# Preparing the inputs inside the first attention: one merged stage with loads three slots ahead, and the bf16 remainders subtracted on VectorE

## The chip, the cores and the metric

The kernel runs on one core of a Trainium2 chip. The metric is the device time of one execution in microseconds (us), the median of the runs shown.

## The reference, cut to what matters

`x` and `ctx_2048` are both 64 x 64 x 256 in fp32. Eight residual stages follow one another, an attention and a feed-forward layer four times. The change touches the first attention and what prepares it; the other seven stages stay as they are.

```
x = x + L0_xattn(layernorm(x), ctx_2048, ctx_2048)          # the stage that is changed
# in it: q is split over its 64 rows into 8 heads of 8 rows, likewise k and v
qk = einsum('bdm,bdn->bmn', qh, kh) / sqrt(8)               # 512 heads, 256 x 256 each
ret = einsum('bmn,bcn->bcm', softmax(qk, axis=-1), vh)
x = x + L0_ffn(layernorm(x), ...)                           # then the other stages
...
x = x + L3_xattn(layernorm(x), ctx_2048, decay, ...)        # uses a decayed sum over the 64 rows of ctx
```

So each of the 64 batches has 8 heads whose contraction is only 8 long, and whose scores are 256 by 256. The kernel keeps fp32 accuracy with bf16 matmuls: an fp32 number is written as the sum of three bf16 numbers (a first part, the rounded remainder, and the remainder of that). Nine products of parts, 8 rows each, give a contraction over 72 partitions.

## The kernel before, in words

One core holds all of `x` in SBUF as `X`, 32 tiles of 128 rows (two batches) by 256. Two functions that run one after the other, with a barrier between them, do what the change touches.

`prepare` runs over 8 groups of 4 tiles (512 rows), two groups a loop turn. For a group SyncE loads `X` and the context `C` (L131, L133). VectorE takes mean and variance (L262, L265), GpSimd the root (L192, L193), VectorE normalises into `Z` (L269). ScalarE casts the first bf16 part of `C` and of `Z` (L234, L237). The remainders of `C` are subtracted on GpSimd (L197, L200), those of `Z` on VectorE (L273, L276), and ScalarE casts the second and third parts (L242 to L248). SyncE stores the three parts of both to DRAM scratch, `z_parts` and `context_parts`, 128 KB an issue (L155, L160). TensorE transposes `C` (L214), ScalarE copies it to `CT` (L240), and 16 narrow matmuls a group (L221) build the decayed sums of the last attention.

`row_attention` runs over 64 units of 8 heads; 4 units make a pair of tiles, and 2 units share one load. Its engines go through the same slots, one unit a slot: in slot n TensorE makes the scores of unit n (L502, two matmuls a head, into a ring of three PSUM banks `psS`), and VectorE takes each row's maximum from that bank (L610). GpSimd splits the maxima into three bf16 parts (L461 to L465), TensorE turns them (L512), ScalarE copies them out (L570), and SyncE brings them into rows 72 to 74 of the query tile `Q9` (L376). Three slots later TensorE makes the shifted scores (L524, into two buffers `psT`), ScalarE takes the exponential (L576), and TensorE multiplies by the values (L537); `V9`, copied from `CT` by GpSimd (L451), carries a column of ones for the denominators. Every fourth slot SyncE stores the sums (L384), fetches the denominators (L390), stores their inverses (L394) and brings both back (L400, L402); GpSimd scales and adds to `X` (L470, L473). SyncE also loads the queries of a later group at odd slots (L364, 576 KB) and its keys at even ones (L370, 3 x 192 KB), two slots before their use for the keys. The middle of both functions is a hardware loop.

All semaphore waits are written by hand, and each engine takes its instructions strictly in the order written. All DMAs are issued by SyncE, so a wait in its queue holds back every later transfer.

## Time and profile before

| | |
|---|---|
| median of 3 runs (lowest to highest) | 2002.18 us (1997.76 to 2004.27) |
| the profiled execution | 2001.07 us |
| its span, first to last instruction | 1999.0 us |
| busy: TensorE, VectorE, ScalarE, GpSimd | 68%, 68%, 56%, 25% of the span |
| mean granted TensorE clock | 0.841 of full speed |
| the last instruction of `prepare` is issued at | about 115 us |
| first score matmul of the attention | 134.88 us |

The span is a chain of stages, so the shares of the whole span say little. The stretch from 0 to about 115 us is `prepare`, from there to about 570 us the first attention. A row of the timeline gives the start in us, how long the instructions merged in it took, engine, line, operation, and in brackets how long the engine had stood idle and for whom.

### The profile page before, as it was taken

The page shows a single profiled execution, that of the slowest core. Times are in us where ns is not written, and L with a number is a line of the kernel's source. Part 1 is how long each engine was busy: PE and PEld are TensorE (multiplying, and loading weights), DVE is VectorE, ACT ScalarE, POOL GpSimd, SP SyncE. Part 2 cuts the span into 40 slices and gives each one's busy share as a digit, 9 for nine tenths or more (in the row PEclk, how much of TensorE's full clock was granted, in tenths as well). Part 3 has the DMA queues.
Part 4 walks back from the last instruction along what each step waited for, and adds up shares of the span by engine and source line. Part 5 has one row for each costly group of instructions (what it writes and reads, how often), then busy time and mean ns, then how long its engine had stood idle before and what let it go on. Part 6 is the DMA issues. An engine that isn't in the chain of part 4 may idle for free. (4 is left out here: it accounts for less than half of the span.)

```text
span 1999.0 us, 33980 instructions
## 1 busy us (share of the span) xinstructions
PE 1352.8 (68%) x11677; PEld 867.7 (43%) x11698; DVE 1357.4 (68%) x2850; ACT 1119.1 (56%) x1552; POOL 494.0 (25%) x903
## 2 busy tenths in 40 slices
PE   4338999999929995888705666459999546774111
PEld 4315555555517773455501333336666423442100
DVE  6646888888624443478767999726666477775896
ACT  4515777777712121677635888724444337775554
POOL 4412233333320004111002443100101011112663
PEclk9999999999959997899955666679999877777555
DMA  5652555555430002333210000011111210000111
GB/s 167 206 128 61 122 132 132 129 131 132 98 92 1 0 1 39 62 76 74 44 66 2 0 1 1 0 56 31 38 44 27 87 31 1 1 1 11 43 53 42
DMA packets 96395, 118.12 MB, mean 59 GB/s; under 512 B 29728, under 2 KB 82152, under 8 KB 91660
## 3 DMA queue, kind: packets, MB, share of 16 engines
q1 hardware_dynamic: 96268, 116.46, 23.3%
q8 instruction: 75, 1.23, 0.3%
q14 instruction: 52, 0.43, 0.1%
HBM read 80.07 MB, written 22.88 MB: 52 GB/s over the span
## 5 line engine op out<-in xcount | busy, mean ns | idle before, releaser
L610 DVE TENSOR_REDUCE ratt_nmax<-ratt_psS 128x2 f32<-128x512 f32 x512 | 318.3, 684 | 97.3 <-PE ratt_psS L502 97.0
L576 ACT ACTIVATE ratt_E<-ratt_psT 128x1024 f32<-128x1024 f32 x256 | 255.0, 1023 | 108.3 <-PE ratt_psT L524 108.2
L502 PE MATMUL ratt_psS<-ratt_K,ratt_Q 72*128 72x256 bf16 x1024 | 204.0, 283 | 41.5 <-DMA ratt_K<-context_parts 35.9
L524 PE MATMUL ratt_psT<-ratt_Q,ratt_K 75*128 75x256 bf16 x1024 | 195.7, 274 | 7.2 <-DMA ratt_Q<-ratt_rows 6.9
L502 PEld LDWEIGHTS ratt_psS<-ratt_K,ratt_Q 72*128 72x128 bf16 x1024 | 79.9, 99 | 137.5 <-issue 66.0
L537 PE MATMUL ratt_psO<-ratt_E,ratt_V 128*32 128x256 f32 x2048 | 137.9, 387 | 0.7 <-ACT ratt_E L576 0.7
L524 PEld LDWEIGHTS ratt_psT<-ratt_Q,ratt_K 75*128 75x128 bf16 x1024 | 99.4, 98 | 25.1 <-DMA ratt_Q<-ratt_rows 7.4
L3405 PE MATMUL final_psT<-final_identh,final_Z 128*128 128x128 f16 x64 | 8.2, 309 | 110.6 <-ACT final_Z L3439 110.6
L537 PEld LDWEIGHTS ratt_psO<-ratt_E,ratt_V 128*32 128x32 f32 x2048 | 53.6, 109 | 50.4 <-issue 27.4
L897 ACT COPY sffn_XS<-sffn_psG 128x512 f32<-128x512 f32 x8 | 4.7, 586 | 125.6 <-PE sffn_psG L846 125.6
L2207 PE MATMUL nffn_psH<-nffn_W,nffn_QT 128*128 128x512 bf16 x121 | 53.2, 586 | 30.6 <-ACT nffn_H L2286 20.0
L2761 DVE SCALAR_TENSOR_TENSOR gffn_H<-gffn_psU,gffn_uwu,gffn_S 128x512 f32<-128x512 f32 x64 | 46.0, 745 | 27.9 <-ACT gffn_S L2936 27.1
L2864 PE MATMUL gffn_psG<-gffn_WG,gffn_QT 128*128 128x512 bf16 x120 | 49.2, 495 | 22.7 <-DVE gffn_H L2761 19.2
L461 POOL TENSOR_TENSOR ratt_parts<-ratt_nmax,ratt_zero 128x16 bf16<-128x16 f32 x64 | 17.2, 269 | 178.4 <-DVE ratt_nmax L610 178.4
L863 PE MATMUL sffn_psH<-sffn_XS,sffn_W 128*128 128x256 f32 x256 | 58.6, 388 | 3.8 <-ACT sffn_XS L897 3.8
L2237 PE MATMUL nffn_psO<-nffn_W,nffn_HT 128*128 128x256 bf16 x256 | 46.1, 340 | 21.1 <-DVE all_X L2126 18.1
L872 PE MATMUL sffn_psO<-sffn_W,sffn_H 128*128 128x256 f32 x256 | 57.4, 382 | 4.4 <-ACT sffn_H L907 4.4
L2400 POOL TENSOR_TENSOR all_X<-all_X,satt_bo 128x1024 f32<-128x1024 f32 x8 | 18.9, 2365 | 167.4 <-DVE all_X L2465 167.4
L214 PE MATMUL prep_psC<-all_ident,prep_C 128*128 128x128 f32 x64 | 15.7, 426 | 60.9 <-DMA prep_C<-in_ctx_dram 58.2
L1273 DVE SCALAR_TENSOR_TENSOR gatt_PB<-gatt_psS,gatt_PB 128x512 f32<-128x512 f32 x64 | 41.2, 686 | 22.0 <-PE gatt_psS L1014 21.7
L3405 PEld LDWEIGHTS final_psT<-final_identh,final_Z 128*128 128x128 f16 x64 | 6.2, 140 | 114.2 <-ACT final_Z L3439 83.3
L2578 ACT COPY satt_AT<-satt_psF 128x256 f32<-128x256 f32 x32 | 11.9, 373 | 76.4 <-PE satt_psF L2515 76.4
(472 smaller groups left out, 3739.7 us busy)
## 6 DMA issues: line engine op xcount, KB each, us to landing
ratt_Q<-z_parts SPq DMA_DIRECT2D x32, 576.0 KB
ratt_K<-context_parts SPq DMA_DIRECT2D x96, 192.0 KB
gatt_V<-in_ctx_dram SPq DMA_DIRECT2D x16, 512.0 KB, 6.7
z_parts<-prep_ZS SPq DMA_DIRECT2D x48, 128.0 KB, 2.6
context_parts<-prep_CS SPq DMA_DIRECT2D x48, 128.0 KB, 2.3
head_sums<-ratt_O SPq DMA_DIRECT2D x64, 72.0 KB
all_X<-in_x_dram SPq DMA_DIRECT2D x8, 512.0 KB
prep_C<-in_ctx_dram SPq DMA_DIRECT2D x8, 512.0 KB
```

The lines of the kernel that those rows point to most:

```text
L502: mm = nc.tensor.matmul(psS[:, RING[h], c * D:(c + 1) * D], Q9[0:R, buf, h, k % 2, c * P:(c + 1) * P], K9[0:R, buf, h, k % 2, :], start=Tr ...
L524: mm = nc.tensor.matmul(psT[:, p % 2, e, c, :], K9[0:RM, buf, h, u, c * P:(c + 1) * P], Q9[0:RM, buf, h, u, :], start=True, stop=True)
L537: mm = nc.tensor.matmul(psO[32 * g:32 * g + 32, q, :], V9[:, b, c, q * 4 + g, :], E[:, 2 * b + q, g, c, :], start=(c == 0), stop=(c == KC ...
L576: nc.scalar.activation(E[:, 2 * b + p // 2, 2 * (p % 2):2 * (p % 2) + 2], psT[:, p % 2], ACT.Exp, scale=SCALE).then_inc(exped, 1)
L610: nc.vector.tensor_reduce(nmax[:, k % 2, h, :], psS[:, RING[h]].rearrange("p (c t) -> p c t", c=2), AX.X, ALU.max, negate=True).then_inc(m ...
L863: mm = nc.tensor.matmul(psH[:, f % 2, ff, :], W1[:, k, c * P:(c + 1) * P], XS[:, k, :], start=(k == 0), stop=(k == KC - 1))
L872: mm = nc.tensor.matmul(psO[:, b, :], H[:, c, b * P:(b + 1) * P], W2[:, c, :], start=(c == 0), stop=(c == FC - 1))
L1273: v.scalar_tensor_tensor(half, heads.psS[:, r].rearrange("p (h t) -> p h t", t=L), float(DH) ** -0.5, half, ALU.mult, ALU.mult).then_inc(h ...
L2207: nc.tensor.matmul(psH[:, j % 2, cols], QT[:, g % 2, k, j * P:(j + 1) * P], W1[:, k, cols], start=(k == 0), stop=False)
L2237: mm = nc.tensor.matmul(psO[:, j % 2, 0:D], HT[:, j % 2, n, :], W2[:, n, :], start=(n == 0), stop=(n == FF // P - 1))
L2761: v.scalar_tensor_tensor(H[:, g % 2, j, h * HALF:(h + 1) * HALF], psU[:, h, :], uwu[:, g % 2, j:j + 1], S[:, h, :], ALU.mult, ALU.mult).th ...
L2864: nc.tensor.matmul(psG[:, h, :], QT[:, g % 2, k * G + j, :], WG[:, k, cols], start=(k == 0), stop=(k == KC - 1))
```

## The change

`prepare` and `row_attention` become one function, `first_attention`, with one set of slots, written out without hardware loops. It begins 12 slots (`LEAD`) before the first unit. A pair of tiles (256 rows) takes the place of the group of four, and the preparation of pair a is spread over the slots that `at(n, r)` names: step r of pair a stands in slot 4a - 12 + r. Its loads stand at r = -3, three slots before its first step. The steps: 1 turn the context on TensorE and copy it (into `psT`, the ring of the shifted scores) and take statistics; 2 aggregate, first part of C, its remainder; 3 root, second part of C; 4 normalise, third part of C, weigh; 5 first part of Z, sums; 6 remainder of Z, second part of Z; 7 third part of Z. The stores follow one slot behind each part (3 to 5 for C, 6 to 8 for Z).

Other work moves between engines: all remainders are subtracted on VectorE, the second parts are cast by GpSimd, the third part is written directly by the subtraction, the normalisation moves to ScalarE, and the decayed sums go from TensorE to GpSimd (a product) and VectorE (a sum). `CS`, `ZS` and `Z` have one buffer each where `prepare` had two of the parts; `C` keeps two. Lines below are those of the kernel before where they begin with a minus.

```
-def prepare(nc, io, X, CT, ident, zq, ck, ST, wsum):
...
-def row_attention(nc, io, X, CT, ident, identb, zq, ck, o_dram, r_dram):
+def first_attention(nc, io, X, CT, ident, identb, zq, ck, o_dram, r_dram, ST, wsum):
...
+    LEAD = 12
...
+        C = s.sb("C", [P, 2, 2, D])
+        Z = s.sb("Z", [P, 2, D])
+        CS = s.sb("CS", [P, 3, 2, D], BF16)
+        ZS = s.sb("ZS", [P, 3, 2, D], BF16)
...
+        def at(n, r):
+            a, left = divmod(n + LEAD - r, 4)
+            return a if left == 0 and is_pair(a) else None
...
+                def load_c(a):
+                    if a > 1:
+                        sp.wait_ge(c_third, a - 1)
...
+                def load_q(g):
+                    pair, b = g // 2, g % 2
+                    sp.wait_ge(z_out, pair * 48 + 48)
...
+                for n in range(-LEAD - 3, UNITS + 11):
+                    if at(n, -3) is not None:
+                        load_x(at(n, -3))
+                        load_c(at(n, -3))
                     if is_unit(n - 1):
+                        bring_row(n - 1)
+                    if n % 2 and is_unit(n + 3):
+                        load_q((n + 3) // 2)
+                    if n % 2 == 0 and is_unit(n + 2):
+                        load_k((n + 2) // 2)
...
+                    for part in range(3):
+                        if at(n, 3 + part) is not None:
+                            store_c(at(n, 3 + part), part)
+                        if at(n, 6 + part) is not None:
+                            store_z(at(n, 6 + part), part)
...
+                def second_of_z(a):
+                    pool.wait_ge(z_rest, a + 1)
+                    gp.tensor_copy(ZS[:, 1], Z[:]).then_inc(z_second, 1)
...
+                def turn_context(a):
+                    j = job["turn", a]
+                    pe.wait_ge(c_in[a % 2], a // 2 * 16 + 16)
+                    if j > 1:
+                        pe.wait_ge(exped, j - 1)
+                    for k in range(KC):
+                        for t in range(2):
+                            mm = nc.tensor.transpose(psT[:, j % 2, 0, k, t * P:(t + 1) * P],
+                                                     C[:, a % 2, t, k * P:(k + 1) * P], ident[:])
...
+                def first_of_z(a):
+                    act.wait_ge(z_done, a * 2 + 2)
+                    if a > 0:
+                        act.wait_ge(z_out, a * 48)
+                    sc.copy(ZS[:, 0], Z[:]).then_inc(z_first, 1)
+                def first_of_c(a):
+                    act.wait_ge(c_in[a % 2], a // 2 * 16 + 16)
+                    if a > 0:
+                        act.wait_ge(c_out, a * 48)
+                    sc.copy(CS[:, 0], C[:, a % 2]).then_inc(c_first, 1)
...
+                def rest_of_c(a):
+                    dve.wait_ge(c_first, a + 1)
+                    dve.wait_ge(written, job["turn", a] + 1)
+                    v.tensor_tensor(C[:, a % 2], C[:, a % 2], CS[:, 0], ALU.subtract).then_inc(c_rest, 1)
```

VectorE's order in the attention, before: eight maxima a unit, and every fourth unit a reciprocal, nothing else.

```order
L610 TENSOR_REDUCE ratt_nmax<-ratt_psS 128x2 x96
L619 RECIPROCAL ratt_inv<-ratt_inv 128x64
L610 TENSOR_REDUCE ratt_nmax<-ratt_psS 128x2 x32
L619 RECIPROCAL ratt_inv<-ratt_inv 128x64
```

The same engine after, over one pair of tiles in the middle of the attention (L574 are the maxima, L581 the reciprocal).

```order
L574 TENSOR_REDUCE ratt_nmax<-ratt_psS 128x2 x8
L566 TENSOR_TENSOR ratt_CS<-ratt_C,ratt_CS 128x512
L574 TENSOR_REDUCE ratt_nmax<-ratt_psS 128x2 x8
L542 BN_STATS ratt_stats<-all_X 128x6 x2
L570 TENSOR_REDUCE all_ST<-ratt_product 128x2x4
L574 TENSOR_REDUCE ratt_nmax<-ratt_psS 128x2 x8
L549 BN_AGGR ratt_mv<-ratt_stats 128x2 x2
L562 TENSOR_TENSOR ratt_C<-ratt_C,ratt_CS 128x512
L553 TENSOR_TENSOR ratt_Z<-ratt_Z,ratt_ZS 128x512
L574 TENSOR_REDUCE ratt_nmax<-ratt_psS 128x2 x8
L581 RECIPROCAL ratt_inv<-ratt_inv 128x64
L557 TENSOR_TENSOR ratt_ZS<-ratt_Z,ratt_ZS 128x512
```

Between each unit's eight maxima and the next unit's now stand one to four instructions of the preparation; the two subtractions L562 and L553 stand behind one another in the third of the four slots.

SyncE's order before, around the slot that stores the sums (L384).

```order
L376 DMA ratt_Q<-ratt_rows 3x8x128 x2
L370 DMA ratt_K<-context_parts 24x4096 x3
L384 DMA head_sums<-ratt_O 9x4x512 x4
L376 DMA ratt_Q<-ratt_rows 3x8x128 x2
L364 DMA ratt_Q<-z_parts 72x1x4096
L390 DMA ratt_inv<-head_sums 128x1x64
L376 DMA ratt_Q<-ratt_rows 3x8x128 x2
```

The same place after (L214 are the rows, L207 the keys, L221 the sums, L199 the queries, L226 the denominators).

```order
L214 DMA ratt_Q<-ratt_rows 3x8x128 x2
L207 DMA ratt_K<-context_parts 24x4096 x3
L231 DMA inverse_sums<-ratt_inv 128x64
L221 DMA head_sums<-ratt_O 9x4x512 x4
L185 DMA context_parts<-ratt_CS 16x8x512
L190 DMA z_parts<-ratt_ZS 16x8x512
L174 DMA all_X<-in_x_dram 128x2x256
L180 DMA ratt_C<-in_ctx_dram 128x2x256
L214 DMA ratt_Q<-ratt_rows 3x8x128 x2
L199 DMA ratt_Q<-z_parts 72x1x4096
L226 DMA ratt_inv<-head_sums 128x1x64
L185 DMA context_parts<-ratt_CS 16x8x512
```

Behind the sums' stores now stand a pair's second store of C and last store of Z, then the loads of a later pair, and only then the next unit's rows; the last store of C stands behind the query load and the denominators.

ScalarE's order after, over the same four slots from the one with the normalisation (L477 exponential, L491 and L470 the copies of values and rows).

```order
L498 ACTIVATE ratt_Z<-all_X,ratt_shift,ratt_rstd 128x256 x2
L477 ACTIVATE ratt_E<-ratt_psT 128x1024 x2
L491 COPY ratt_O<-ratt_psO 128x2x256
L483 COPY all_CT<-ratt_psT 128x2x256
L477 ACTIVATE ratt_E<-ratt_psT 128x1024
L470 COPY ratt_rows<-ratt_psS 48x128
L477 ACTIVATE ratt_E<-ratt_psT 128x1024
L505 CAST ratt_ZS<-ratt_Z 128x512
L477 ACTIVATE ratt_E<-ratt_psT 128x1024 x2
```

A cast that waits for the stores of the pair before (L505, and one slot later L511 for C) now stands between one unit's last exponential and the next unit's first.

## Rows read from the trace of the kernel before

**Rows 1.** Stages by windows: us, busy PE, PEld, DVE, ACT, POOL, PEclk, DMA, GB/s.

```profile
0.00:60.00 60.00, 22.22 (x104) 21.95 (x105) 37.43 (x73) 30.31 (x35) 23.39 (x30) 1.00 0.58 175
300.00:400.00 100.00, 98.04 (x1043) 59.33 (x1040) 81.11 (x133) 74.83 (x97) 34.19 (x104) 1.00 0.55 131
```

**Rows 2.** Timeline, from the end of the preparation to the first shifted scores.

```profile
111.44 3.85 SPq L160 DMA_DIRECT2D context_parts<-prep_CS  x6
...
123.69 1.50 SPq L370 DMA_DIRECT2D ratt_K<-context_parts  x3
...
134.88 3.17 PE L502 MATMUL ratt_psS<-ratt_K,ratt_Q 72*128 72x256 bf16 x12 [32.67 <-DMA ratt_K<-context_parts]
...
157.13 0.61 PE L524 MATMUL ratt_psT<-ratt_Q,ratt_K 75*128 75x256 bf16 x2 [6.90 <-DMA ratt_Q<-ratt_rows]
```

**Rows 3.** Timeline of ScalarE, VectorE and TensorE over two slots of the attention.

```profile
327.40 1.02 ACT L576 ACTIVATE ratt_E<-ratt_psT 128x1024 f32<-128x1024 f32 x1 [0.17 <-PE ratt_psT L524]
...
329.38 1.94 ACT L576 ACTIVATE ratt_E<-ratt_psT 128x1024 f32<-128x1024 f32 x2 [0.96 <-PE ratt_psT L524]
...
331.39 0.38 PE L524 MATMUL ratt_psT<-ratt_Q,ratt_K 75*128 75x256 bf16 x2
...
333.58 1.02 ACT L576 ACTIVATE ratt_E<-ratt_psT 128x1024 f32<-128x1024 f32 x1 [0.17 <-PE ratt_psT L524]
...
334.91 2.48 DVE L610 TENSOR_REDUCE ratt_nmax<-ratt_psS 128x2 f32<-128x512 f32 x4 [0.84 <-PE ratt_psS L502]
...
335.81 0.38 PE L502 MATMUL ratt_psS<-ratt_K,ratt_Q 72*128 72x256 bf16 x2
```

**Rows 4.** Timeline: the first context has landed.

```profile
7.16 1.05 ACT L234 CAST prep_CS<-prep_C 128x1024 bf16<-128x1024 f32 x1 [2.95 <-DMA prep_C<-in_ctx_dram]
```

**Rows 5.** Lines before 640 us, the prices: busy us, mean ns, idle before.

```profile
L200 POOL TENSOR_TENSOR prep_CR<-prep_CR,prep_CS 128x1024 f32<-128x1024 f32 x8 | 17.0, 2121 | 34.5 <-ACT prep_CS L242 34.5
...
L214 PE MATMUL prep_psC<-all_ident,prep_C 128*128 128x128 f32 x64 | 15.7, 426 | 60.9 <-DMA prep_C<-in_ctx_dram 58.2 <-ACT all_CT L240 2.7
...
L273 DVE TENSOR_TENSOR prep_ZR<-prep_Z,prep_ZS 128x1024 f32<-128x1024 f32 x8 | 9.8, 1226 | 8.9 <-ACT prep_ZS L237 8.9
...
L262 DVE BATCH_NORM_STATS2 prep_stats<-all_X 128x6 f32 x24 | 8.4, 407 | 0.0
L237 ACT CAST prep_ZS<-prep_Z 128x1024 bf16<-128x1024 f32 x8 | 8.4, 1044 | 35.5 <-DVE prep_Z L269 35.5
...
L193 POOL TENSOR_TENSOR prep_rstd<-prep_veps,prep_mhalf 128x4 f32<-128x4 f32 x8 | 8.1, 1012 | 0.6
```

**Rows 6.** Page: DMA issues, KB each, median us to landing.

```profile
z_parts<-prep_ZS SPq DMA_DIRECT2D x48, 128.0 KB, 2.6
context_parts<-prep_CS SPq DMA_DIRECT2D x48, 128.0 KB, 2.3
```

**Rows 7.** Timeline of SyncE over the same two slots.

```profile
324.93 2.73 SPq L384 DMA_DIRECT2D head_sums<-ratt_O  x4
327.76 1.51 SPq L376 DMA_DIRECT2D ratt_Q<-ratt_rows  x2
329.57 0.90 SPq L364 DMA_DIRECT2D ratt_Q<-z_parts  x1
330.86 0.61 SPq L390 DMA_DIRECT2D ratt_inv<-head_sums  x1
```

**Rows 8.** Two single lines: L390's time to landing, and L269's durations (min/median/max).

```profile
DMA to landing us min/median/max: 2.0/4.8/5.4
...
L269 DVE TENSOR_SCALAR prep_Z<-all_X,prep_mv,prep_rstd x32: 399/402/2206, 9.7 to 102.3; 128x256 f32 x24, 128x256 f32<-128x256 f32 x8
```

**Rows 9.** Windows of 1 us around the query load of Rows 7.

```profile
330.00:331.00 1.00, 1.00 (x19) 0.42 (x16) 1.00 (x3) 1.00 (x2) 0.00 (x0) 1.00 0.09 21
...
334.00:335.00 1.00, 1.00 (x17) 0.54 (x10) 0.16 (x2) 0.61 (x1) 0.69 (x3) 1.00 0.38 87
335.00:336.00 1.00, 1.00 (x11) 0.88 (x10) 1.00 (x2) 0.43 (x1) 0.57 (x3) 1.00 0.03 7
```

**Rows 10.** Timeline: a GpSimd and a VectorE subtraction side by side in the preparation.

```profile
93.14 2.12 POOL L200 TENSOR_TENSOR prep_CR<-prep_CR,prep_CS 128x1024 f32<-128x1024 f32 x1 [4.34 <-ACT prep_CS L242]
94.00 2.34 DVE L276 TENSOR_TENSOR prep_ZR<-prep_ZR,prep_ZS 128x1024 f32<-128x1024 f32 x1 [1.74 <-ACT prep_ZS L244]
```

More of the change, by code:

```diff
@@ L427, in _ @@
[L427 to L434 removed]
+                        to = o_dram.rearrange("a (w g) c m -> a g c w m", g=4)[a, g]
@@ new lines, in _ @@
+                gp.memset(flip[:], 0.0).then_inc(ready, 1)
+                gp.memset(ones[:], 1.0).then_inc(ones_set, 1)
+                pool.wait_ge(ready, 7)
+                for n in range(2):
+                    gp.affine_select(out=flip[:], in_=flip[:], compare_op=ALU.not_equal, fill=1.0,
+                                     base=1 - L - n * L, pattern=[[1, L]], channel_multiplier=1).then_inc(ready, 1)
+                    pool.wait_ge(ready, 8 + n)
+                gp.memset(zero[:], 0.0).then_inc(v_set, 1)
@@ L485, in _ @@
-                slots(pool, slot, UNITS + 14)
+                        split_max(n - 1)
+                    if n % 4 == 1 and is_pair(n // 4 - 4):
+                        scale_and_add(n // 4 - 4)
+                    if at(n, 3) is not None:
+                        root(at(n, 3))
+                        second_of_c(at(n, 3))
+                    if at(n, 4) is not None:
+                        weigh(at(n, 4))
+                    if at(n, 6) is not None:
+                        second_of_z(at(n, 6))
@@ L562, in _ @@
-                slots(pe, slot, UNITS + LAG + 1)
+                            turn_max(n - 1)
             @block.scalar
             def _(act):
-                def row(u, b, half):
-                    act.wait_ge(turned, u + 1)
-                    if past(u, 2):
-                        act.wait_ge(row_in[b], half * 32)
-                    nc.scalar.copy(rows[:, b, :], psM[0:6 * NH0]).then_inc(row_out, 1)
-                def exp(m, b, p):
-                    act.wait_ge(shifted, m * 4 + (p + 1))
-                    if p == 0 and past(m, 2):
-                        act.wait_ge(pv, m - 1)
-                    nc.scalar.activation(E[:, 2 * b + p // 2, 2 * (p % 2):2 * (p % 2) + 2], psT[:, p % 2], ACT.Exp,
-                                         scale=SCALE).then_inc(exped, 1)
@@ L579, in leave, with row @@
[L579 to L588 removed]
+                sc = nc.scalar
+                def row(n):
+                    act.wait_ge(turned, n + 1)
+                    if n > 1:
+                        act.wait_ge(row_in[n % 2], n // 2 * 32)
+                    sc.copy(rows[:, n % 2, :], psM[0:6 * NH0]).then_inc(row_out, 1)
@@ L589, in slot @@
+                sc.activation(keep[:, 0:1], decay[:], ACT.Exp, scale=-1.0).then_inc(expd, 1)
+                for n in range(-LEAD, UNITS + LAG + 1):
                     m = n - LAG
```

672 lines of the change are left out of this document (306 added, 366 removed).

## The prediction

> **What bounds the kernel now.** I read the windows by stage first, then the timeline across the border between the two functions, then one period of four slots engine by engine. In the preparation no engine is near full: VectorE is busiest with 37.43 of 60 us, TensorE has 22.22 [rows 1]. In the attention TensorE is busy 98.04 of 100 us, VectorE 81.11, ScalarE 74.83, GpSimd 34.19, the DMA engines 0.55 [rows 1]. So the attention is bound by TensorE, and the preparation by its chain of small steps. Between them lies a border: the last store is issued by 115.3 us, the first keys are issued by 125.19, the first score runs at 134.88, and the first shifted score at 157.13 after waiting 6.90 us for its rows [rows 2]. A slot takes 333.58 - 327.40 = 6.18 us from one unit's last exponential to the next one's [rows 3], four of them 24.7.
>
> **What the change removes.** The first score no longer waits for all 16 pairs, only for pair 0 and for what is queued ahead of it. Its chain: context and statistics wait for the load and the weights, done by 7.2 us [rows 4]. Then transposes 1.0, a copy and the first part of C 0.52 each (half of L237's 1044 ns), remainder 0.62 (half of L273), second part on GpSimd 1.1 (half of L200, the nearest row; no row shows such a cast), third part 0.62 [rows 5], two loads and the store 1.5, landing 2.3 [rows 6]: 15.4 us. CS has one buffer, so C's first part of pair 1 waits for that landing; and since VectorE takes C of pair 1 ahead of Z of pair 0, Z of pair 0 waits too: 0.52 + 0.62 + 0.62, GpSimd's Z part 1.1, root 1.8 (1012 ns and three small ones), C part 1.1, third part 0.6: 21.8. Store, loads and landing of Z 4, query and key issue 2.4, landing near 4: 32 us. Bounds: 26, if the root (1.8) is done while others wait and the Z store and the keys land 2.0 sooner each, and 46, if the first keys take the 9.7 us that they took from the end of their issue (125.19) to the first score [rows 2]. Saved: 134.9 - 32 = 103 us (89 to 109). Of the 6.90 us for the first rows I take 4 as gone (0 to 6.9): behind the first loads now stand fewer transfers. Together 107.
>
> **What it adds to a period.** Pairs 3 to 15 prepare beside running units: 13 periods. I call the four slots A (the sums are stored), B, C and D; B is the one whose last exponential starts at 327.40 [rows 3].
>
> *Transposes (B).* 64 took 15.7 us [rows 5], so four take 1.0 on the engine that bounds. 0.5 if half falls into its own waits, 1.5 if the extra job in the ring of two psT buffers holds the next one up. I take 1.0. The 128 narrow matmuls for the sums leave TensorE, but from a stage where it had time: nothing.
>
> *First part of Z (end of B).* ScalarE now waits there until all Z stores of the pair before have landed, with every later exponential behind it. SyncE issues the last of these behind the sums' stores, which end at 324.93 + 2.73 = 327.66 [rows 7]; two stores of 0.64 each (six took 3.85) [rows 2], and 2.6 to land [rows 6]: 331.5. ScalarE's slot B ends at 327.40 + 1.02 = 328.4, with the transposes 329.4. It waits, casts 0.52, and starts slot C's exponentials at 332.0 in place of 329.38 + 1.0. That is 1.6 late; the shifted score that needs the first of them stood at 331.39, 1.0 after that one's end (half of the 1.94) [rows 3]. TensorE loses 0.6. It is 0 if the store lands a microsecond sooner, and about 3 if it lands as L390's load does, at 4.8 (median) to 5.4 us [rows 8].
>
> *Remainder of C (end of C).* SyncE in slot B: the stores end at 328.9, two loads 0.9, rows 1.5, then the query load waits for the same landing, 331.5; query 0.9, denominators 0.6 [rows 7], last store of C 0.64: 333.6. Its data stand behind the 576 KB of the query, which before was issued by 330.5 and kept the DMA engines busy until about 334.5 [rows 7, 9]: landing near 336.9. ScalarE's slot C ends at 333.58 + 1.02 + 1.6 = 336.2; it waits 0.7, casts 0.52: 337.4. VectorE waits for that cast, then subtracts twice, 2 x 0.62, and only then takes slot D's first maximum, at 338.7 in place of 334.91 + 1.6 = 336.5. The score that needs that bank free starts at 335.81, 0.28 after the first maximum's end (0.62 long, a quarter of 2.48) [rows 3]; so 2.2 - 0.3 = 1.9 lost. Bounds 0.5 (the landing is early; the cast and two subtractions remain) and 4.4 (it comes 2.5 later).
>
> *The rest of VectorE.* B gains two statistics and a sum, 0.7 + 0.6; A and D a subtraction of 0.62 each [rows 5]. VectorE has 0.84 idle in a slot ahead of a first maximum [rows 3], which hides A and D; B overruns by a few tenths. I take 0.5 (0 to 2.3). ScalarE's copy and normalisation and GpSimd's casts fall into idle time: nothing, if GpSimd's split of the maxima is not late; what it costs otherwise is in the bounds of VectorE.
>
> Sum: 1.0 + 0.6 + 1.9 + 0.5 = 4.0 a period, 13 x 4.0 = 52 us. The keys are not late next: SyncE is done with B by 333.6, before slot C's rows are ready, so C's keys are issued no later than now. The loop's end had held SyncE and TensorE up by tenths only; written out, I count it as nothing.
>
> The profiled execution took 2001.1: 2001.1 - 107 + 52 = 1946. It lies 1.1 under the median of 2002.2, so 1947 is the forecast, 2.7% faster. Its own range, from the bounds that are near: 1932 to 1962.
>
> **A page against the rows.** L276, which starts at 94.00 beside L200 on GpSimd (93.14 to 95.26), took 2.34 us where the same subtraction in L273 took 1226 ns; a normalisation L269 took up to 2206 ns against a median of 402 [rows 5, 8, 10]. "SBUF — State Buffer" of the Trainium skill (section "SBUF: two separate sides") says that VectorE with two SBUF inputs and GpSimd share a port pair which the first to start holds for its whole instruction. By that rule the trace agrees, and moving subtractions to VectorE makes them a party to it. It becomes the second rival below.
>
> **Rivals.**
>
> 1. *The covers hold: only the transposes and half a microsecond remain.* For it: the DMA engines are down to 0.09 when the sums have been stored [rows 9], so the stores may land early enough. Against: the two subtractions behind a fresh cast stand in the order whatever the landing. 13 x 1.5 = 20: 2001.1 - 107 + 20 = 1914, with the median 1915.
> 2. *VectorE is held by GpSimd.* A subtraction that meets a GpSimd instruction waits for most of it, as L276 did by 1.1 us [rows 5, 10]. Two such a period, beyond the cover, make 2.3: 13 x 2.3 = 30, so 1977. For it: GpSimd gains two casts and a product a pair. Against: in the order GpSimd waits for the subtraction itself in slot C, and so is idle beside it.
> 3. *Slower: the single buffers make each landing a stall.* ZS and CS cannot be written before three stores have landed, and ScalarE stands in front of all exponentials while it waits. The loss passes the 107 saved at 107 / 13 = 8.2 us a period, 4.2 more than I count. Both landings add in full once ScalarE is waiting, so it decides from 2.1 us more each, that is 4.7 for Z. For it: L390's load takes 4.8 in this very stretch [rows 8], and the first rows waited 6.90 behind loads [rows 2]. Against: these stores took 2.6 beside a DMA share of 0.58, higher than the attention's 0.55 [rows 1, 6]. With 2.5 more each it is 9.0 a period: 2001.1 - 107 + 117 = 2011, median 2012.
> 4. *The early start doesn't come.* The three leading pairs wait for one another's landings, and the first score comes at 46 or later, and the rows wait as before: 18 of the saving lost, 1965. For it: all in one SyncE queue. Against: the units run once pair 0 is there. It is mostly inside my range.
>
> **How the numbers follow.** Forecast 0.52 (1947), rival 1 0.15 (1915), rival 2 0.12 (1977), rival 3 0.11 (2012), rival 4 0.10 (1965). A change of under 0.3%, 6 us, can't be told from none here. From rivals 2 and 3 I leave some chance near the old time: same 0.03, slower 0.10, faster 0.87. The range of 8 in 10 is 1914 to 1988: it leaves out rival 3 and a tail of rival 1.
>
> **What would show it.** The first score near 32 us (26 to 46); a period of four units at 24.7 + 4.0 = 28.7 us while pairs are prepared and 24.7 in the last ones; four transposes in B; ScalarE waiting for `z_parts` at the end of B by about 2 us and for `context_parts` at the end of C by under 1; VectorE's gap before D's first maximum; the first attention ending some 55 us earlier; every later stage as long as now. Wrong it is if the first score comes after 46, if a period is under 26 or over 32 us, or if the stalls stand on GpSimd or on the keys.

## The result, and the profile after

Over 20 runs of each on one chip the changed kernel took 2006.15 us (median; 1993.16 to 2014.65) and the kernel before 1998.76 (1994.68 to 2005.13). The ratio is 1.0031, with a 95% interval of 1.002 to 1.0042: slower by 0.3%, where 2.7% faster was forecast. The profiled execution took 2004.2 us (span 2002.5) against 2001.07 (span 1999.0).

| | before | forecast | changed kernel |
|---|---|---|---|
| first score, us | 134.88 | 32 (26 to 46) | 33.79 |
| first shifted score, us | 157.13 | 50 (157.13 - 107) | 51.08 |
| mean period of four units while pairs are prepared, us | 25.1 | 28.7 | 34.2 |
| ScalarE's last copy of the first attention, us | 556.85 | some 55 earlier | 559.84 |
| granted TensorE clock, 300 to 400 us | 1.00 | (not treated) | 0.85 |

The mean period is the distance between SyncE's loads of the numerators (`ratt_num`), one a pair, over ten pairs: (490.20 - 148.08) / 10 after, (488.03 - 236.72) / 10 before. All that follows the first attention takes as long as it did: its end moved by 3.0 us and the whole by 3.1.

The two scores in the changed kernel's timeline answer to [rows 2]. The start came 106 us earlier, as forecast (107):

```profile
33.79 3.18 PE L387 MATMUL ratt_psS<-ratt_K,ratt_Q 72*128 72x256 bf16 x12 [17.01 <-DMA ratt_K<-context_parts]
...
51.08 0.64 PE L405 MATMUL ratt_psT<-ratt_Q,ratt_K 75*128 75x256 bf16 x2
```

The window of the changed kernel that answers to [rows 1] (columns as there). TensorE is busy 84.98 us of 100 in place of 98.04, at a granted clock of 0.85 in place of 1.00; VectorE and ScalarE, which were given the added work, are busy less than before too. Something holds everything up:

```profile
300.00:400.00 100.00, 84.98 (x769) 48.41 (x771) 70.93 (x124) 61.45 (x86) 37.96 (x98) 0.85 0.55 134
```

Where TensorE loses its time is told by the sums of its own waits between 100 and 420 us (engine, what it does, what it waits for, us, times, longest). The kernel before hardly waits for the maxima (first line); the changed kernel waits 3.8 us a time for them, and 1.2 for the exponentials:

```profile
PE ratt_psS L502 <- DVE ratt_nmax L610: 1.1, 3, 0.6
...
PE ratt_psS L387 <- DVE ratt_nmax L574: 34.1, 9, 5.1
...
PE ratt_psT L405 <- ACT ratt_E L477: 10.5, 9, 1.7
```

What holds it up stands in the timeline of the two slots that answer to [rows 3] and [rows 7]: the end of slot B (312), of slot C (319) and the start of slot D. Columns: start, us, engine, line, operation, and in brackets the idle time ahead of it and what ended it.

```profile
301.26 0.68 DVE L566 TENSOR_TENSOR ratt_CS<-ratt_C,ratt_CS 128x512 bf16<-128x512 f32 x1
...
308.11 1.47 SPq L190 DMA_DIRECT2D z_parts<-ratt_ZS  x1
...
312.27 0.62 ACT L505 CAST ratt_ZS<-ratt_Z 128x512 bf16<-128x512 f32 x1 [3.45 <-DMA z_parts<-ratt_ZS]
...
313.87 0.39 PE L405 MATMUL ratt_psT<-ratt_Q,ratt_K 75*128 75x256 bf16 x2 [1.74 <-ACT ratt_E L477]
...
314.24 0.60 SPq L185 DMA_DIRECT2D context_parts<-ratt_CS  x1
316.28 1.55 SPq L214 DMA_DIRECT2D ratt_Q<-ratt_rows  x2
...
319.24 0.62 ACT L511 CAST ratt_CS<-ratt_C 128x512 bf16<-128x512 f32 x1 [2.07 <-DMA context_parts<-ratt_CS]
319.89 0.69 DVE L562 TENSOR_TENSOR ratt_C<-ratt_C,ratt_CS 128x512 f32<-128x512 f32 x1 [3.33 <-ACT ratt_CS L511]
320.50 0.68 DVE L553 TENSOR_TENSOR ratt_Z<-ratt_Z,ratt_ZS 128x512 f32<-128x512 f32 x1
321.10 2.48 DVE L574 TENSOR_REDUCE ratt_nmax<-ratt_psS 128x2 f32<-128x512 f32 x4
321.25 0.61 POOL L312 CAST ratt_ZS<-ratt_Z 128x512 bf16<-128x512 f32 x1 [11.32 <-DVE ratt_Z L553]
321.85 0.60 PE L387 MATMUL ratt_psS<-ratt_K,ratt_Q 72*128 72x256 bf16 x2 [1.79 <-DVE ratt_nmax L574]
...
327.79 1.57 SPq L214 DMA_DIRECT2D ratt_Q<-ratt_rows  x2
```

Read it from the last store of C at 314.24. It lands at 319.2; ScalarE has waited 2.07 us for it and casts; VectorE has waited 3.33 us for the cast, subtracts twice and only then, at 321.10, comes to slot D's first maximum; TensorE has waited 1.79 us for that maximum, less than in any other period (3.1 to 5.1 us in the ten others between 100 and 460 us). GpSimd stands behind VectorE's second subtraction as well, 11.32 us, with a copy of values and a split of maxima queued behind; the list of waits has none of TensorE for the rows that this split leads to. And the data of that store were ready at 301.94 already, when VectorE had written the third part (L566). From one unit's rows to the next (L214) it takes 11.51 us here, 316.28 to 327.79, where one slot took 6.18 before. Five of the 9.1 us that the period grew are in this one slot.

These stores land later than those of [rows 6] (the page's issues: KB each, median us to landing):

```profile
context_parts<-ratt_CS SPq DMA_DIRECT2D x48, 128.0 KB, 4.9
z_parts<-ratt_ZS SPq DMA_DIRECT2D x48, 128.0 KB, 4.9
```

And TensorE's granted clock, the column ahead of the DMA share in windows of 1 us, falls in this period at 316, behind TensorE's idle time at the end of slot B, and comes back in slot D:

```profile
313.00:314.00 1.00, 0.13 (x2) 0.12 (x3) 0.00 (x0) 1.00 (x2) 0.00 (x0) 1.00 0.14 38
...
316.00:317.00 1.00, 1.00 (x16) 0.35 (x8) 0.56 (x3) 1.00 (x3) 0.00 (x0) 0.63 0.94 236
317.00:318.00 1.00, 1.00 (x8) 0.51 (x5) 0.00 (x0) 0.18 (x1) 0.00 (x0) 0.50 0.56 145
...
325.00:326.00 1.00, 1.00 (x7) 0.69 (x6) 0.68 (x1) 0.40 (x1) 0.85 (x3) 0.50 0.04 12
...
327.00:328.00 1.00, 1.00 (x17) 0.59 (x20) 1.00 (x2) 1.00 (x3) 0.00 (x0) 1.00 0.00 0
```

In between, TensorE works at 1.2 GHz in place of 2.4: a pair of score matmuls takes 0.60 us in place of 0.38, and the line "TensorE is busy" hides it.

This period is the exception. The clock falls eleven times between 100 and 460 us, and the ten other times it falls while TensorE waits at the end of slot C, as in the period around 386:

```profile
386.00:387.00 1.00, 0.00 (x0) 0.00 (x0) 0.00 (x0) 0.10 (x1) 0.00 (x0) 1.00 0.48 111
387.00:388.00 1.00, 0.00 (x0) 0.00 (x0) 0.45 (x1) 1.00 (x2) 0.00 (x0) 0.97 0.89 270
388.00:389.00 1.00, 0.00 (x0) 0.00 (x0) 1.00 (x3) 0.45 (x1) 0.08 (x1) 0.50 0.95 219
```

### The profile page after: what moved, and what is told of

It reads as the page before. It is cut to its first block and busy times, and to the rows that moved or that the text cites. A ratio compares the mean times of both kernels' runs of the same rounds, so it can differ in the third digit from the quotient of the medians.

```text
span 2002.5 us, 32075 instructions
## 1 busy us (share of the span) xinstructions
PE 1372.6 (69%) x11551; PEld 856.8 (43%) x11572; DVE 1356.8 (68%) x2881; ACT 1104.0 (55%) x1568; POOL 516.8 (26%) x983
## 5 line engine op out<-in xcount | busy, mean ns | idle before, releaser
L574 DVE TENSOR_REDUCE ratt_nmax<-ratt_psS 128x2 f32<-128x512 f32 x512 | 322.6, 685 | 89.4 <-PE ratt_psS L387 84.4
L477 ACT ACTIVATE ratt_E<-ratt_psT 128x1024 f32<-128x1024 f32 x256 | 256.7, 1024 | 106.0 <-PE ratt_psT L405 105.8
L387 PE MATMUL ratt_psS<-ratt_K,ratt_Q 72*128 72x256 bf16 x1024 | 220.0, 302 | 70.1 <-DVE ratt_nmax L574 46.4
L405 PE MATMUL ratt_psT<-ratt_Q,ratt_K 75*128 75x256 bf16 x1024 | 211.7, 293 | 13.9 <-ACT ratt_E L477 13.9
L387 PEld LDWEIGHTS ratt_psS<-ratt_K,ratt_Q 72*128 72x128 bf16 x1024 | 85.7, 104 | 172.2 <-DVE ratt_nmax L574 100.3
L429 PE MATMUL ratt_psO<-ratt_E,ratt_V 128*32 128x256 f32 x2048 | 157.5, 431 | 0.7 <-ACT ratt_E L477 0.7
L405 PEld LDWEIGHTS ratt_psT<-ratt_Q,ratt_K 75*128 75x128 bf16 x1024 | 105.5, 105 | 41.3 <-ACT ratt_E L477 18.2
L864 PEld LDWEIGHTS sffn_psH<-sffn_XS,sffn_W 128*128 128x128 f32 x256 | 49.2, 195 | 12.5 <-issue 3.0
L344 POOL TENSOR_TENSOR ratt_parts<-ratt_nmax,ratt_zero 128x16 bf16<-128x16 f32 x64 | 23.1, 360 | 122.1 <-DVE ratt_nmax L574 122.1
```

The lines of the kernel that those rows point to most:

```text
L387: mm = nc.tensor.matmul(psS[:, RING[h], c * D:(c + 1) * D], Q9[0:R, buf, h, n % 2, c * P:(c + 1) * P], K9[0:R, buf, h, n % 2, :], start=Tr ...
L405: mm = nc.tensor.matmul(psT[:, j % 2, e, c, :], K9[0:RM, buf, h, u, c * P:(c + 1) * P], Q9[0:RM, buf, h, u, :], start=True, stop=True)
L429: mm = nc.tensor.matmul(psO[32 * g:32 * g + 32, q, :], V9[:, m % 2, c, q * 4 + g, :], E[:, m % 2 * 2 + q, g, c, :], start=(c == 0), stop=( ...
L477: sc.activation(E[:, m % 2 * 2 + p // 2, 2 * (p % 2):2 * (p % 2) + 2], psT[:, j % 2], ACT.Exp, scale=SCALE).then_inc(exped, 1)
L574: v.tensor_reduce(nmax[:, n % 2, h, :], psS[:, RING[h]].rearrange("p (c t) -> p c t", c=2), AX.X, ALU.max, negate=True).then_inc(maxed, 1)
L864: mm = nc.tensor.matmul(psH[:, f % 2, ff, :], W1[:, k, c * P:(c + 1) * P], XS[:, k, :], start=(k == 0), stop=(k == KC - 1))
```

## The experiments

Twelve kernels, run beside the kernel before. Periods are mean periods as above, over the first ten pairs whose loads are seen. The runs were on three occasions, on which the kernel before took 2002.2 to 2002.8 (1998.76 in the result above), so kernels of different occasions are best compared by their ratios. Period and clock are those of the one profiled execution, which lies up to 12 us off the kernel's median (e8): spread over 13 periods that is 0.9 us, so a difference of under 1 us between two periods can be chance.

| run | edit | time, us | ratio to before (95%) | period, us | clock 300:400 |
|---|---|---|---|---|---|
| (changed kernel) | | 2006.15 | 1.0031 (1.002 to 1.0042) | 34.2 | 0.85 |
| e1_parts | a semaphore for each store of ZS and CS | 1938.96 | 0.9696 (0.968 to 0.9713) | 28.4 | 0.98 |
| e2_parts_z | the same for ZS alone | 2011.41 | 1.0054 (1.0032 to 1.0075) | 34.1 | 0.89 |
| e3_parts_c | the same for CS alone | 1945.94 | 0.972 (0.9704 to 0.9736) | 29.4 | 0.98 |
| e4_fill | matmuls without use where TensorE idles | 1993.72 | 0.9953 (0.9935 to 0.9972) | 33.2 | 0.90 |
| e5_order_c | C's last store one slot earlier | 1945.94 | 0.9723 (0.9697 to 0.9749) | 28.9 | 1.00 |
| e6_later | e1, and C's remainder a slot later | 1925.62 | 0.9615 (0.9581 to 0.9648) | 27.5 | 0.97 |
| e7_pool | the subtractions on GpSimd | 1947.64 | 0.9735 (0.9708 to 0.9763) | 28.4 | 0.98 |
| e8_loads0 | loads at the pair's own slot | 1988.83 | 0.9931 (0.9907 to 0.9955) | 31.9 | 0.88 |
| e9_rest_later | C's remainder a slot later, alone | 1944.93 | 0.9719 (0.9687 to 0.975) | 28.8 | 0.97 |
| e10_best | e6, and the sums' stores a slot earlier | 1915.54 | 0.9567 (0.9544 to 0.9591) | 27.1 | 0.98 |
| e11_best2 | e10, and the loads one slot ahead | 1919.3 | 0.9587 (0.9558 to 0.9617) | 26.9 | 1.00 |
| e12_act_queue | C's last store from ScalarE's queue | 1963.33 | 0.981 (0.9786 to 0.9834) | 30.3 | 0.95 |

### Take the landing waits away: e1, e2, e3

The waits can go without another buffer: a first cast needs only the first store's place to be free, and that store was issued two slots before the third.

```diff
-                        act.wait_ge(c_out, a * 48)
+                        act.wait_ge(c_out[0], a * 16)
+                        act.wait_ge(c_rest, a)
```

GpSimd's and VectorE's writes wait for the second and third store likewise, and SyncE's loads for all three.

> The changed kernel with one edit: each of the three stores of ZS and of CS gets its own semaphore, so the first cast of a pair waits only for the first store of the pair before (issued two slots earlier), not for all three. Theory A (ScalarE stands before its casts until the last store has landed, 35.0 us in 12 waits for z_parts and 29.0 in 13 for context_parts, and TensorE's idle behind it lets the granted clock fall): both waits go to under 0.3 us a period, the granted clock is 1.00 from 120 to 560 us as in the kernel before, the period of four units falls from 33.0 to 27 to 28 us (24.7 + 1.0 of transposes + about 2 of subtractions behind a fresh cast), 13 periods x 5 to 6 = 65 to 78 us: 2006 becomes 1928 to 1945. Theory B (the added work on VectorE and TensorE fills the slots, the landings only show where the time would be lost anyway): period 31 to 33, time 1985 to 2006. Theory C (the wait moves to the query loads, which need all three stores): ScalarE's waits go, TensorE waits for ratt_Q by as much, time 1985 or more.

Measured: 1938.96, inside theory A's 1928 to 1945; both waits are gone from the list. The period of 28.4 and the clock of 0.98 just miss what it said. B and C fall. The window (columns as above):

```profile
300.00:400.00 100.00, 90.72 (x937) 53.81 (x938) 85.34 (x151) 75.50 (x102) 45.16 (x118) 0.98 0.68 162
```

> The same edit for ZS alone, so that the wait for context_parts at the end of slot C stays. Theory A with stalls that each carry their own fall of the clock: the period falls by about half of what both edits give, to 30 us, time 1965 to 1972. If one stall is enough to hold the clock down for half of the period: only the 2.2 us of the wait itself go, period 31, time 1975 to 1982, and both edits together give more than the sum of the two alone. Theory B: 1995 to 2006.

> The same edit for CS alone, so that the wait for z_parts at the end of slot B stays. Theory A with stalls that each carry their own fall of the clock: period 30 us, time 1965 to 1972. If the Z stall alone takes the clock down (it falls at 316, four microseconds behind TensorE's idle at 312 to 314, and before the C stall begins): the clock stays under 0.9 in this kernel, period 30.5 to 31, time 1975 to 1982, while the edit for ZS alone gives more. Theory B: 1995 to 2006.

Measured: 2011.41 for ZS alone, 1945.94 for CS alone. Neither form of theory A had this: the two stalls are not halves. Without the Z wait ScalarE is at C's cast earlier, and the store that it waits for lands no earlier, so that wait takes the time. The sums of the waits between 100 and 420 us (columns as above), first of the changed kernel:

```profile
ACT ratt_CS L511 <- DMA context_parts<-ratt_CS: 22.8, 9, 3.7
```

then of e2_parts_z:

```profile
ACT ratt_CS L517 <- DMA context_parts<-ratt_CS: 39.3, 9, 6.2
```

That is 2.5 us a time before the edit and 4.4 after; TensorE's wait for the maxima grows with it, from 34.1 us in 9 to 50.5 in 9. Without the C wait (e3), the Z wait stays, 31.1 us in 11, and costs 29.4 - 28.4 = 1.0 us a period against e1 in the profiled executions; the medians differ by 7 us, which makes 0.5. The clock of e3 is 0.98, so the Z stall alone doesn't hold it down. So the fault is at the end of slot C.

### What the clock costs: e4

```diff
+    FILL = (14, 14)
...
+                            if (n % 4, p, e) == (3, 1, 1) and is_unit(n) and is_unit(m):
+                                fill(psO[:, 1, :], n, FILL[1])
                             if is_unit(n):
                                 score(n, 2 * p + e)
+                            if (n % 4, p, e) == (2, 2, 0) and is_unit(n) and is_unit(m):
+                                pe.wait_ge(maxed, n * NH0 + 3)
+                                fill(psS[:, 2, 0:D], n, FILL[0])
```

> The changed kernel with both waits left in, and 14 matmuls of 256 columns without use (into banks that are free at the time) in TensorE's queue at each of its two idle places of a period: 14 x 0.11 = 1.5 us each at full clock, where TensorE stood idle for 1.74 and 1.79. It separates the stall from the fall of the clock. Theory A with the clock as a part of its own: the granted clock is back near 1.00, ScalarE's waits for z_parts and context_parts stay at 2 to 3 us each, and the period falls from 33.0 to 28.5 to 30 us, 2006 to 1945 to 1970. If the clock costs little (TensorE waits for others anyway): time within 0.5% of 2006, or above it by the fill, up to 13 x 3 = 39 us more.

Measured: 1993.72. It misses the first forecast by 24 us and lies 2 us below the second. The waits stayed (28.5 us in 10 for Z, 23.0 in 10 for C), the clock came back only in part, and the period fell by 1.0:

```profile
300.00:400.00 100.00, 93.26 (x883) 57.52 (x880) 73.50 (x128) 64.00 (x89) 38.71 (x101) 0.90 0.57 140
```

With useless work TensorE is busy 93.26 us, and the ratio is 0.9953 where the changed kernel's is 1.0031, 0.8% faster: the clock has a price of its own, but it follows from the stall. A mean of 0.85 means 30% of the time at 1.2 GHz, some 10 us a period. About 2 us of these TensorE idles, so I estimate up to 4 us a period lost there, against 1 in e9 (0.97). The fill, which does not reach 1.00, confirms no more than 1.0 of it; and e2 has the same period, 34.1, at a clock of 0.89.

### Why C's store comes so late: e5, e8, e12

The third part of C is ready at 301.94, and its store is issued at 314.24: in SyncE's order it stands behind the keys, the sums' stores, Z's store, the loads of a later pair, the next rows and the query. e5 moves it up; nothing else changes.

```diff
-                        if at(n, 3 + part) is not None:
+                        if part < 2 and at(n, 3 + part) is not None:
                             store_c(at(n, 3 + part), part)
...
+                    if at(n, 4) is not None:
+                        store_c(at(n, 4), 2)
```

> The changed kernel, buffers and semaphores as they are, with the third store of C issued one slot earlier on SyncE, right behind the third store of Z (in place of after the next rows, the query load and the denominators). The edit of the semaphores for CS alone had given 1946, for ZS alone 2011. Theory A2 (the C stall is what sets the period, and it is long because SyncE comes to C's last store late, at 314.24, though the data are there since about 303): the store goes out near 309.7, lands near 314.6, before ScalarE is done with slot C at 317.2; the wait for context_parts goes to under 0.5 us a period, the one for z_parts stays near 2.8, period 29, time 1940 to 1955. Rival D (the landing is long because of what the DMA engines carry, and grows with an earlier issue): landing 6 to 9 us, the wait stays above 1.5, time above 1975.

Measured: 1945.94, period 28.9, as A2 said, and the same time as with the semaphores for CS (e3); D falls. SyncE's timeline in e5; the store of C in the second line is the one that stood at 314.24:

```profile
308.61 0.76 SPq L190 DMA_DIRECT2D z_parts<-ratt_ZS  x1
309.41 0.60 SPq L185 DMA_DIRECT2D context_parts<-ratt_CS  x1
```

ScalarE's wait for C is gone from the list, the one for Z stays (30.9 us in 11).

e8 puts the loads back from three slots ahead to the pair's own slot:

```diff
-                    if at(n, -3) is not None:
+                    if at(n, 0) is not None:
```

> The changed kernel with the other number of the change moved: the loads of x and of the context at the pair's own slot instead of three slots ahead. It takes the 512 KB from the place just behind the third store of Z and puts them a few slots later in the queue. Theory A2: the landings stay at 4.5 to 5, the period at 34, the time within 0.5% of 2006, if the loads, which landed in 3.6 us, come before the statistics. Rival F (these loads are what delays the landing of C's last store): its landing falls by a microsecond or more and the time to under 1990. If the loads come too late: VectorE or ScalarE waits for x or ctx, over 2016.

Measured: 1988.83, outside of what A2 said. It is the time that F gave, but not for F's reason: the landing did not change (median 4.8). What changed is the moment: SyncE has two issues fewer between Z's last store and C's, and the wait for it is half as long (11.5 us in 10, from 22.8 in 9):

```profile
ACT ratt_CS L511 <- DMA context_parts<-ratt_CS: 11.5, 10, 2.6
```

e12 issues that store from ScalarE's own queue:

```diff
                     if at(n, 5) is not None:
+                        store_c(at(n, 5), 2)
                         first_of_z(at(n, 5))
```

> The changed kernel with the third store of C issued from ScalarE's queue, ahead of its first part of Z, in place of SyncE's, so that nothing of SyncE's stands ahead of it. It asks why the stores land in 4.9 us where they took 2.3 to 2.6 before. If it is the place in SyncE's queue, behind 72 KB stores and 256 and 576 KB loads: this store lands in 2 to 3 us while the others stay at 5. If it is the load of the DMA engines as a whole (share 0.55): it lands in 4 to 5. In either case it is issued some 5 us earlier, before 310 where it was 314.24, so the wait for context_parts goes and the time is that of the kernel with the earlier store, 1940 to 1960, with 13 x 0.1 to 0.6 us for the issue on ScalarE in it.

Measured: 1963.33, slower than e5 and outside the 1940 to 1960. The wait for C is gone, the one for Z grew to 40.3 us in 11. The DMA issues of that kernel between 100 and 420 us:

```profile
context_parts<-ratt_CS SPq DMA_DIRECT2D x21, 128.0 KB, 5.1
...
context_parts<-ratt_CS ACTq DMA_DIRECT2D x10, 128.0 KB, 4.0
```

A queue of its own brings at most 1.1 us; the landing stays at 4.0, so most of the delay is not SyncE's queue. Nor is it sure that the queue brings the 1.1: in e5, which issues this store at nearly the same point of the period from SyncE (309.41; here 309.70), the median over all stores of C is 4.0 too. What the longer landing comes from stays open.

### Who carries the stall to TensorE: e7, e9

e7 undoes the second part of the change: the four subtractions are GpSimd's again, the merged stages stay.

```diff
                     if at(n, 3) is not None:
                         root(at(n, 3))
+                        rest_of_c(at(n, 3))
                         second_of_c(at(n, 3))
                     if at(n, 4) is not None:
+                        third_of_c(at(n, 4))
                         weigh(at(n, 4))
                     if at(n, 6) is not None:
+                        rest_of_z(at(n, 6))
                         second_of_z(at(n, 6))
+                    if at(n, 7) is not None:
+                        third_of_z(at(n, 7))
```

The same four calls leave VectorE's order.

> The changed kernel with its second part undone: the four subtractions of a pair on GpSimd instead of VectorE (the remainder of C just ahead of GpSimd's second part). All waits of ScalarE for landings stay. Theory A2 (the C stall reaches TensorE through VectorE, which stands in front of the next maxima behind the cast): VectorE no longer waits for the cast, TensorE's wait for nmax goes, and the C stall costs TensorE no more than the Z stall does; period 30 to 32, time 1960 to 1985, if GpSimd is not late with the split of the maxima. If ScalarE's late exponentials alone carry the stall: 1998 to 2012. If GpSimd, with 4 x 1.1 us more a period, becomes late with its split: over 2012.

Measured: 1947.64, better than theory A2 had it, with both waits of ScalarE still there (between 100 and 420 us):

```profile
ACT ratt_ZS L527 <- DMA z_parts<-ratt_ZS: 35.3, 12, 3.4
...
ACT ratt_CS L533 <- DMA context_parts<-ratt_CS: 25.4, 11, 3.2
```

TensorE's wait for the maxima is gone from the list, and the one for the exponentials has grown to 24.3 us in 21. So the late landings cost much less by themselves. Either VectorE was short of time, or it stood in the wrong place (GpSimd's remainder of C stands a slot later than VectorE's did). e9 tells these apart with one line; the subtractions stay on VectorE:

```diff
-                    if at(n, 2) is not None:
-                        rest_of_c(at(n, 2))
+                    if at(n, 3) is not None:
+                        rest_of_c(at(n, 3))
```

> The changed kernel with one line moved: VectorE's remainder of C stands one slot later in its order, at the end of slot D in place of the end of slot C; buffers, semaphores, stores and ScalarE's two waits for landings stay as they are. The kernel with the subtractions on GpSimd (1948) kept both waits too (35.3 us in 12, 25.4 in 11) and had a period of 28.1. Theory A3 (what costs is VectorE standing behind the late cast, ahead of the eight maxima of a slot; ScalarE's own waits cost TensorE little): period 28 to 29, TensorE's wait for nmax under 1 us a period, granted clock 0.95 or more, time 1940 to 1955. Rival G (GpSimd helped because it took 2.7 us of subtractions a period off VectorE): period 31 or more, time 1970 to 2006.

Measured: 1944.93, period 28.8, clock 0.97, all as A3 said. Rival G falls. The timeline of e9 at the end of slot C and through slot D (columns as above):

```profile
307.54 1.56 SPq L214 DMA_DIRECT2D ratt_Q<-ratt_rows  x2
...
307.74 0.66 DVE L553 TENSOR_TENSOR ratt_Z<-ratt_Z,ratt_ZS 128x512 f32<-128x512 f32 x1
...
308.57 2.48 DVE L574 TENSOR_REDUCE ratt_nmax<-ratt_psS 128x2 f32<-128x512 f32 x4 [0.18 <-PE ratt_psS L387]
...
310.57 0.62 ACT L511 CAST ratt_CS<-ratt_C 128x512 bf16<-128x512 f32 x1 [2.13 <-DMA context_parts<-ratt_CS]
...
314.57 1.58 SPq L214 DMA_DIRECT2D ratt_Q<-ratt_rows  x2
...
315.08 0.63 DVE L562 TENSOR_TENSOR ratt_C<-ratt_C,ratt_CS 128x512 f32<-128x512 f32 x1
```

The cast is as late as before, with 2.13 us of wait ahead of it, but VectorE is at slot D's maxima 2 us ahead of it and takes the remainder at 315.08, when the cast is long done. From rows to rows it is 7.03 us in place of 11.51. TensorE's waits between 100 and 420 us, which were 10.5 us in 9 for the exponentials and 34.1 in 9 for the maxima:

```profile
PE ratt_psT L405 <- ACT ratt_E L477: 20.0, 19, 1.7
...
PE ratt_psS L387 <- DVE ratt_nmax L574: 3.2, 9, 0.4
```

Of the 34.2 - 28.8 = 5.4 us a period that e9 gives back, 3.4 are TensorE's wait for the maxima, and 0.7 go back into its wait for the exponentials: 2.7 net. The other 2.7 fit the 3 us of clock estimated under e4, but no run shows them by themselves. ScalarE's waits are not harmless either: e6 below, without them, is 1.0% faster than e9 (and has two more parts of C moved).

### A version that beats both: e6, e10, e11

e6 joins e1 and a later remainder, with what follows it a slot later too:

```diff
+    C_AT = (3, 5, 6)
...
-                        if at(n, 3 + part) is not None:
-                            store_c(at(n, 3 + part), part)
+                        if at(n, C_AT[part]) is not None:
+                            store_c(at(n, C_AT[part]), part)
...
-                    if at(n, 2) is not None:
-                        rest_of_c(at(n, 2))
-                    if at(n, 4) is not None:
-                        third_of_c(at(n, 4))
+                    if at(n, 3) is not None:
+                        rest_of_c(at(n, 3))
+                    if at(n, 5) is not None:
+                        third_of_c(at(n, 5))
```

and GpSimd's `second_of_c` from `at(n, 3)` to `at(n, 4)`.

> The kernel with a semaphore for each store of ZS and CS (1939), and besides it the remainder of C one slot later on VectorE, with the second and the third part of C a slot later behind it. It takes away the subtraction behind a fresh cast, which after the landings is what is left of slot C's stall: VectorE waited 10.1 us in 11 for that cast and TensorE 12.4 in 11 for the maxima in a window of 320 us. Theory A: 13 x 1.0 to 1.3 = 13 to 17 us less, 1920 to 1928. Rival: the keys, for which TensorE waited 15.6 us in 15 in that window, take the time instead: 1933 to 1940.

Measured: 1925.62, inside theory A's range, though TensorE now waits for keys. Both its own waits and its weight loads' (100 to 420 us):

```profile
PEld ratt_psS L398 <- DMA ratt_K<-context_parts: 20.1, 17, 2.7
...
PE ratt_psS L398 <- DMA ratt_K<-context_parts: 12.2, 11, 2.2
```

e10 moves the four stores of the sums out of SyncE's full stretch, to the end of the slot before:

```diff
-                        if is_pair(c):
-                            out(c)
...
+                    if n % 4 == 3 and is_pair(n // 4 - 1):
+                        out(n // 4 - 1)
```

> The kernel with a semaphore for each store and the remainder of C a slot later (1926), and besides it the four stores of the sums of a pair at the end of the slot before on SyncE (which has 6 us without an issue there, 342.53 to 348.59 in the kernel with a semaphore for each store), so that the run of 20 issues without a gap behind it gets shorter by 2.7 us and the keys are issued earlier. If the keys, for which TensorE waited 12.2 us in 11 there (and its weight loads 20.1 in 17), are late because SyncE is late: this goes, 13 x 1.1 to 1.5 = 14 to 20 us less, 1906 to 1912. If the keys wait for the DMA engines' own load (share 0.66): 1918 to 1926.

Measured: 1915.54, between the two forecasts. The keys' wait fell from 12.2 us in 11 to 9.2 in 13, and did not go:

```profile
PE ratt_psS L398 <- DMA ratt_K<-context_parts: 9.2, 13, 1.6
```

e11 has the loads at `at(n, -1)` in place of `at(n, -3)` as well:

> The kernel before this one with the loads of x and of the context in the slot ahead of the pair's own, where SyncE has its gap, in place of three slots ahead (two slots before, which is in the full stretch). If SyncE's full stretch still makes keys or query late: another 5 to 10 us less, 1898 to 1907. If nothing waits for SyncE any more: within 0.3% of the kernel before this one. If the statistics or the transposes wait for the loads: slower by up to 13 us.

Measured: 1919.3; the intervals of e10 and e11 overlap, so no effect of the loads' place is shown. TensorE still waits for keys, 14.3 us in 16; what they wait for stays open. e10 has the lowest time: 4.3% under the kernel before.

## Why the prediction was wrong, step by step

**The early start: right.** First score at 33.79 (32), first shifted score 106 us earlier (107). Rival 4 fell. The bound of 46 does not follow from its own condition: with 9.7 in place of 4 for the first keys the sum gives 38.

**The step that failed: "Remainder of C (end of C)", 1.9 us a period with bounds of 0.5 and 4.4.** Moving that one subtraction out of its place (e9) gives back 34.2 - 28.8 = 5.4 us a period in the ten that were measured, and 2006 becomes 1945, two below my forecast. The mechanism was in the text: the landing, the cast, VectorE behind it, two subtractions, then the maxima. Three of its sizes were off.

- The landing: I let the store land 3.3 us after its issue (333.6 to 336.9); here it took 5.0, 314.24 to 319.2, with a median of 4.9. ScalarE's wait became 2.07 us instead of 0.7 (2.5 in the mean).
- The place in SyncE's order: I priced the order as it stood and did not ask what stood ahead of a store whose data were ready. e5 gains 60 us by that order alone.
- TensorE's clock: I counted all work at 2.4 GHz. It fell to half for some 10 us of each period, in ten of eleven while TensorE stood idle at the end of C.

The Trainium skill gives, in "DMA: Bandwidth & Descriptors" (section "Anatomy of one DMA — SWDGE (gpsimd) path"), about 2.0 us plus the bytes at 436 GB/s, a fit to DMAs issued by GpSimd; for 128 KB that makes 2.3 as an estimate. In the preparation the trace agrees (2.3 for C, 2.6 for Z, [rows 6]), in the attention it does not (4.9). The same page of the Trainium skill says in "Latency and other measured facts" that HBM takes longer under load; the trace shows the later landing, but no run here separates that cause.

**First part of Z: 0.6 foreseen, 0.5 to 1.0 measured** (e3 against e1, by the medians and by the periods), inside its bounds of 0 to 3. The intervals of the two kernels overlap, so it is hardly clear of the noise. Its wait was longer than counted (2.8 us a time), and one-sided: taken away alone it gave nothing.

**Transposes and the rest of VectorE: not contradicted, not shown.** e7 takes the four subtractions off VectorE and e9 keeps them; their ratios, 0.9735 and 0.9719, don't differ beyond their intervals. So where the subtractions don't stand in the way no cost is seen, against the 0.5 counted. The four transposes of a pair take 0.66 us on TensorE (L417 at 304.89) against the 1.0 counted; no run leaves them out. With C's remainder out of the way a period is still 28.8 - 25.1 = 3.7 us longer than before, where the sum without C's 1.9 had 2.1.

**The rivals.** Rival 3 came nearest: single buffers turn landings into stalls, 2012 against 2006. But its price was put equally on both landings, and nearly all of it is C's. What it lacked is the part between: ScalarE's waits of 2.9 and 2.3 us a time remain in e7, and 58 of the 59 us that my forecast was short do not (2006 to 1948). Nor does it take a second buffer: a narrower wait (e1) or another order (e5, e9) was enough. Rival 2 did not show: of the 64 subtractions two took 1.7 us (L566, ahead of the first unit), all others 0.63 to 0.69, and e7 differs from e9 by 0.1%. Rival 1's 1915 was reached by e10 alone, with three more edits.

**What would make it wrong: right.** "A period over 32" is what came, at the place named: the ends of B and C. The 0.87 for faster left rival 3 little because these stores had landed in 2.6 us at a higher DMA share; in the attention they took 4.9, and C's bound of 4.4 also took the clock as fixed. With 5.4 in place of 1.9, and 1.0 for Z in place of 0.6, the same sum gives 4.0 + 3.5 + 0.4 = 7.9 a period; 9.1 were measured. Where the other 1.2 lies isn't settled; e6, e10 and e11 take the period from 28.8 down to 26.9, and in them TensorE still waits for keys.

## What to carry to other kernels

When work is merged into a full pipeline, price each added instruction by what stands behind it in its engine's order, not by its length: 0.69 us of subtraction ahead of the maxima, behind a fresh cast, cost 5.4 us a period, clock included, and one slot later TensorE's wait for the maxima was 0.3. For a buffer that is stored in parts, wait for the part and not for the whole, and issue a store when its data are ready; neither took a buffer here (e1, e5). And when one of two waits is removed without gain, look for the other one getting longer before calling it harmless.

## What the runs showed of the hardware that was not expected

- The same 128 KB stores land in 2.3 to 2.6 us beside the preparation and in a median of 4.9 beside the attention, at nearly the same DMA share (0.58 and 0.55). From ScalarE's queue it was 4.0, and 4.0 too for C's stores from SyncE's queue in e5 (the median over all three parts). The Trainium skill says in "DMA: Bandwidth & Descriptors" (section "Issuing engines are not separate DMA queues") that issuing from several engines saves only the sequencer's time; that ScalarE's queue was no faster than SyncE's in e5 agrees with it.
- The granted clock of TensorE went from 1.00 to 0.50 once a period, for some 10 us: in ten of eleven periods within an idle time of 3.1 to 5.1 us, in one behind an idle time of 1.74 us that had ended at 313.87. Useless matmuls in the idle places made the whole kernel 0.8% faster than without them.
- GpSimd's cast of 128x512 to bf16 (L312 above) takes 0.61 us, about half of the 1.1 that I took from its subtraction.
